# Vision tower on one Trainium2 core: TensorE's fused stage as a loop over two pairs, gelu into its own tile, spectra of the rows loaded for two pairs

## The chip, the cores and the metric

One core of a Trainium2 chip runs the whole program. The metric is the device time of one execution in microseconds, as the median of several runs. "PE" is TensorE (matmuls; "PEld" its weight loads), "DVE" VectorE, "ACT" ScalarE, "POOL" GpSimd, "SP" SyncE, which here only issues transfers.

## The reference

The input is a batch of 64 images of 64 x 64 pixels with 3 channels. The first block is a Fourier network of width 64 with four layers. Around it follow a linear attention, a mixture of experts, a second attention and a second mixture of experts on the tokens; the change does not touch those. Each of the four layers computes, cut to what matters:

```
xf  = rfft2(h)                                   # h: [b, 64, 64, 64]
top = einsum('bixy,ioxy->boxy', xf[:, :, :16, :16], w1)
bot = einsum('bixy,ioxy->boxy', xf[:, :, -16:, :16], w2)
sc  = irfft2(of)                                 # of: zeros, with top and bot in place
pw  = einsum('bihw,oi->bohw', h, pw_w[l]) + pw_b[l]
y   = sc + pw
h   = gelu(batchnorm(y))                         # over batch and pixels, for each channel
```

After the last layer comes `gelu(h @ fc1_w + fc1_b) @ fc2_w + fc2_b`, which gives one number for each pixel.

## The kernel before

All transforms are matmuls with small constant matrices in float32. A layer has two stages. The **mix** stage takes the spectra of all images, 8 chunks of modes one after the other, multiplies them with the layer's weights and stores the products in `spec_out` (in DRAM). It also gathers the sums for the batch norm from the spectra, so that scale and shift are known before any pixel is.

The **fused** stage (`sync_fuse`, `tensor_fuse`, `scalar_fuse`, `vector_fuse`) goes over the 32 pairs of images (`NP = 32`). For each pair it has these steps, each of the pixel steps in four quarters T = 0 to 3:

- `rows` (matmuls on L896, two halves, `hc` 0 and 1): inverse transform over the rows, read from the tile `grp`, transposed by `turn_rows` (DVE, L915) into `a2`.
- `y_of` with `spectral` (L906): inverse transform over the columns; in layer 0 with the pointwise part of the input on top (L1037); in layers 1 and 2 `add_p` (DVE, L923) adds the pointwise part, which was loaded from `y_dram`.
- `gelu` (ACT, L1132 in layer 0, L1135 later), with the batch norm as scale and shift, in place in the pair's tile `pb`.
- `px_turn` (DVE, L1185) transposes it into `hT`; `next_of` (PE, L1064) multiplies it with the next layer's pointwise weights; `evict` (ACT, L1142) copies that result over the gelu in `pb`; `square` (ACT, L1149) sums its squares; SP stores it to `y_dram` (L943, four transfers of 512 KB).
- `w_dft` (L1077), `w_turn`, `h_dft` (L1090), `h_turn` (L1204): the forward transform, whose result SP stores for every four pairs (`store_spectra`, L972, four transfers of 512 KB).

The order is written out by hand on each engine, and the engines meet at semaphores. On PE the loop over the pairs is unrolled in Python; the only loop of the program is the one over layers 1 and 2 (L2418 on PE). In PE's step n the order is: `next_of(n-1, 2)`, `y_of(n, 0)`, `y_of(n, 1)`, `rows_of(n+1, 0)`, `h_dft(n-2)`, `next_of(n-1, 3)`, `y_of(n, 2)`, `rows_of(n+1, 1)`, `w_dft(n-1)`, `next_of(n, 0)`, `next_of(n, 1)`, `y_of(n, 3)`. The half `rows_of(n+1, 1)` waits until `evict` has ended for pair n-1:

```
if hc == 1 and p > 1:
    pe.wait_ge(evicted, n * 4 - 4)
```

SP issues nearly all transfers in one order that is written out too. `grp` has two buffers (`grp[g % 2]`), each for the spectra of a group of four pairs; `load_piece` brings the next group in four pieces of 512 KB, one in each of SP's steps, by way of `load_group`. A step of SP is: a piece of spectra, every fourth time `store_spectra`, then `store(n-1)`, which waits for the same `evicted` count as the half of `rows` above, then `load(n+2)`, a plane of 2 MB from `y_dram` (L876; in layer 0 two transfers of 48 KB from the input, L880).

The last layer (`sync_last`, `tensor_last`) has neither stores nor forward transforms; it goes on to the two layers `fc1` (L1320) and `fc2` (L1332).

Of the kernel before, what the change touches and what calls it, by code (L numbers as in the profile page):

```python
# [114 lines left out]
def build(nc, d, B, out):  # L115
# [5 lines left out]
    with ExitStack() as ctx:  # L121
# [7 lines left out]
        spec_out = nc.dram_tensor("spec_out", [NCH, P, NG, GI * C], F32, kind="Internal").ap()  # L129
# [354 lines left out]
        m_sb = [at(M_AT + u * (2 * B * HB + 8 * BK), NG, 2, GI * HB) for u in range(2)]  # L484
# [44 lines left out]
        def sync_mix(sp, l, first, final=False):  # L529
# [8 lines left out]
            def store(c):  # L538
                sp.wait_ge(mixed_turned, (l * NCH + c) * 4 + 4)
                sp.sem_inc(waited[sp.engine], 1)  # L540
                for t in range(4):
                    row = t % 2 * C + t // 2 * HB
                    if c >= NCH - 2:
                        sp.dma_start(grp[0].rearrange("p (c v) b o -> p c (v b o)", v=2)[row:row + HB, c],
                                     m_sb[c % 2][t * HB:(t + 1) * HB, 0].rearrange("p v x -> p (v x)")).then_inc(grp_loaded[0], 16)
                if c == NCH - 2:
                    for u in range(2):
                        sp.wait_ge(mixed_stored[u], l * (NCH * 32) + (NCH * 32 - 64))
                        sp.sem_inc(waited[sp.engine], 1)
                    load_group(sp, l, 0, slice(0, NCH - 2))  # L550
# [167 lines left out]
        def vector_mix(dve, l, first):  # L718
# [38 lines left out]
            def turn(n):  # L757
# [11 lines left out]
                for j in range(2):  # L769
                    dve.transpose(m_sb[c % 2][:, 4 * j:4 * j + 4, v, :], modes[:, 32 * j:32 * j + 32]).then_inc(mixed_turned, 1)  # L770
# [59 lines left out]
        grp_loaded = [sem("grp_loaded_even"), sem("grp_loaded_odd")]  # L830
# [9 lines left out]
        grp = [at(u * PX, M2, GI, HB) for u in range(2)]  # L840
# [28 lines left out]
        GRP_LOADS = [(NG // 2 - 1) * Q + 9, NG // 2 * Q]  # L869

        def grp_count(l, g):

            return l * (GRP_LOADS[g % 2] * 16) + ((g // 2 * Q + (9, Q)[g % 2]) * 16)

# [8 lines left out]
        def load_piece(sp, l, n):  # L883
            if n // Q + 1 < NG:
# [1636 lines left out]
```

## Time and profile before

| what | value |
|---|---|
| median of 3 runs | 4079.1 us (4076.56 to 4083.73) |
| the profiled execution's own time | 4098.0 us |
| its span, first to last instruction | 4096.2 us |
| mean granted TensorE clock | 0.909 of full |
| PE busy | 3206.6 us (78%) |
| PE weight loads busy | 1856.2 us (45%) |
| DVE busy | 2414.7 us (59%) |
| ACT busy | 2249.3 us (55%) |
| data moved by the queue that SP fills | 774.61 MB, 61.9% of 16 engines' span |

The times of the runs and the profiled execution are not the same execution: durations below are of the profiled one. The page of the profile shows busy time for each engine and groups of instructions by line. The fused stages lie at 264 to 904 us (layer 0), 1120 to 1737 (layer 1), 1953 to 2569 (layer 2) and 2782 to 3379 (last layer), the mix stages ahead of each. In a timeline a row stands for instructions of one kind that follow each other; in brackets is how long the engine stood idle before the row and what ended that. "issue" means that nothing the profile shows was waited for. The count behind the x is in hardware instructions: one float32 matmul of the code is two of them, so a half of `rows` is 8 matmuls in the code and 16 in the trace.

### The profile page before, as it was taken

What the parts mean: (1) busy time and instruction counts of PE and PEld (TensorE: products, weight loads), DVE (VectorE), ACT (ScalarE), POOL (GpSimd) and SP (SyncE); (2) the same over time, 40 slices, a digit from 0 to 9 for tenths busy, and PEclk for the clock granted to TensorE, in tenths of its full rate; (3) what the DMA queues carried; (4) which work ended last, traced back from release to release, by engine and by line L of the source; (5) the groups of instructions that cost most, each with busy time, mean ns of one, the idle gap of its engine ahead of it and who ended that gap; (6) DMA issues with size and microseconds to landing.
All of it is one profiled execution on the core that took longest, in us unless ns stands there. A gap on an engine that the chain in (4) does not pass through costs nothing. (4 is left out here: it accounts for less than half of the span.)

```text
span 4096.2 us, 119274 instructions
## 1 busy us (share of the span) xinstructions
PE 3206.6 (78%) x52804; PEld 1856.2 (45%) x52804; DVE 2414.7 (59%) x2482; ACT 2249.3 (55%) x2652; POOL 173.7 (4%) x249
## 2 busy tenths in 40 slices
PE   6678888886677777867777777678999994869786
PEld 4544444444544444446444444464444442733532
DVE  4555555555677778856778877564333333554556
ACT  3655565665566566656656666565666663222321
POOL 2013200000000000000000000000010012000000
PEclk9899999998899999988899999898999997779688
DMA  8877766668878889888889988886434320011062
GB/s 284 321 207 184 180 157 154 166 159 296 282 246 257 259 237 279 240 308 297 247 240 273 280 253 230 291 303 219 168 127 162 131 86 12 1 43 42 1 118 60
DMA packets 174127, 798.69 MB, mean 195 GB/s; under 512 B 32137, under 2 KB 38609, under 8 KB 124270
## 3 DMA queue, kind: packets, MB, share of 16 engines
q1 hardware_dynamic: 161628, 774.61, 61.9%
q0 software_dynamic: 7936, 13.65, 1.1%
q8 instruction: 425, 6.96, 0.7%
q10 hardware_dynamic: 4050, 2.74, 0.2%
q14 instruction: 88, 0.72, 0.1%
HBM read 445.01 MB, written 342.23 MB: 192 GB/s over the span
## 5 line engine op out<-in xcount | busy, mean ns | idle before, releaser
L906 PEld LDWEIGHTS bank<-fb,arena 64*64 64x64 f32 x16384 | 558.6, 196 | 548.1 <-issue 491.7
L906 PE MATMUL bank<-fb,arena 64*64 64x128 f32 x16384 | 622.6, 290 | 201.3 <-issue 146.5
L923 DVE TENSOR_TENSOR arena<-bank,arena 128x1024 f32<-128x1024 f32 x384 | 467.7, 1218 | 426.6 <-PE bank L906 425.9
L1142 ACT ACTIVATE arena<-bank 128x1024 f32<-128x1024 f32 x384 | 384.0, 1023 | 535.0 <-PE bank L1064 313.3
L1185 DVE STREAM_TRANSPOSE arena<-arena 128x1024 f32<-128x1024 f32 x384 | 458.4, 1212 | 136.7 <-ACT arena L1132 134.8
L915 DVE STREAM_TRANSPOSE arena<-bank 128x1024 f32<-128x1024 f32 x256 | 318.7, 1245 | 327.7 <-PE bank L896 327.4
L1064 PE MATMUL bank<-arena,wst 64*64 64x512 f32 x3072 | 420.1, 631 | 24.3 <-issue 16.6
L1149 ACT ACTIVATE arena<-arena 128x1024 f32<-128x1024 f32 x384 | 403.1, 1050 | 0.3
L1135 ACT ACTIVATE arena<-arena,shift,scale 128x1024 f32<-128x1024 f32 x256 | 316.5, 1236 | 116.1 <-DVE arena L923 114.4
L896 PE MATMUL bank<-arena,ga 64*64 64x256 f32 x4096 | 304.2, 405 | 94.4 <-DVE arena L923 28.4
L637 PE MATMUL bank<-arena 64*64 64x128 f32 x8192 | 276.0, 282 | 92.9 <-issue 63.8
L1090 PE MATMUL bank<-arena,ghq 32*64 32x256 f32 x6144 | 235.6, 419 | 94.4 <-issue 83.2
L637 PEld LDWEIGHTS bank<-arena 64*64 64x64 f32 x8192 | 249.5, 140 | 130.3 <-issue 128.2
L1320 PE MATMUL bank<-arena,fc 64*128 64x512 f32 x1024 | 274.6, 635 | 18.9 <-ACT arena L1388 18.9
L1388 ACT ACTIVATE arena<-bank,fc1b 128x1024 f32<-128x1024 f32 x256 | 272.3, 1101 | 19.6 <-PE bank L1320 19.5
L896 PEld LDWEIGHTS bank<-arena,ga 64*64 64x64 f32 x4096 | 166.4, 139 | 214.4 <-issue 146.4
L754 DVE SCALAR_TENSOR_TENSOR arena<-bank,arena 128x1024 f32<-128x1024 f32 x128 | 156.3, 1223 | 178.0 <-ACT arena L696 177.4
L1380 ACT ACTIVATE arena<-arena,shift,scale 128x1024 f32<-128x1024 f32 x128 | 158.8, 1241 | 183.1 <-DVE arena L923 183.1
L1204 DVE STREAM_TRANSPOSE arena<-bank 128x512 f32<-128x512 f32 x192 | 196.9, 1106 | 98.3 <-PE bank L1090 98.2
L1077 PE MATMUL bank<-arena,fwq 32*32 32x512 f32 x6144 | 240.0, 609 | 16.1 <-issue 13.6
L1192 DVE STREAM_TRANSPOSE arena<-bank 128x1024 f32<-128x1024 f32 x192 | 231.7, 1220 | 21.7 <-PE bank L1077 21.7
L615 PE MATMUL bank<-arena,wst 64*64 64x256 f32 x1536 | 161.4, 447 | 105.4 <-ACT arena L676 73.8
(240 smaller groups left out, 3641.2 us busy)
## 6 DMA issues: line engine op xcount, KB each, us to landing
y_dram<-arena SPq DMA_DIRECT2D x384, 512.0 KB, 8.2
arena<-y_dram SPq DMA_DIRECT2D x96, 2048.0 KB
spec_out<-arena SPq DMA_DIRECT2D x128, 512.0 KB, 10.6
arena<-in_w_modes SPq DMA_DIRECT2D x28, 2048.0 KB, 14.9
arena<-spec_out SPq DMA_DIRECT2D x112, 512.0 KB, 10.9
arena<-spec_in SPq DMA_DIRECT2D x24, 2048.0 KB, 9.7
spec_in<-arena SPq DMA_DIRECT2D x96, 512.0 KB, 8.4
spec_in<-arena SPq DMA_DIRECT2D x8, 2048.0 KB, 13.4
```

The lines of the kernel that those rows point to most:

```text
L637: mm = pe.matmul(bank[4 * v + q][ROW[h], k * 2 * B:(k + 1) * 2 * B], w_sb[c % 3][ROW[row], mode, :], z[ROW[row], :, :, mode, :], start=(sw ...
L896: mm = pe.matmul(bank[2 * s + v][CHAN[par], :].rearrange("p (c r k) -> p r k c", c=16, r=2)[:, r], ga[k_p, r * S:(r + 1) * S], grp[p // Q ...
L906: mm = pe.matmul(hpx(bank[2 * s + i][CHAN[v], :])[:, :, j * S:(j + 1) * S], a2[p % 2][CHAN[i], :, v, 4 * T + j], hpx(fb2[CHAN[i], :]), sta ...
L915: dve.transpose(a2[p % 2].rearrange("p (v c) a m -> p v (c a m)", v=2)[:, :, hc * 512:(hc + 1) * 512], slot(s)).then_inc(rows_turned, 1)
L923: dve.tensor_tensor(chunk(p, T), slot(s), chunk(p, T), ALU.add).then_inc(y_added, 1)
L1064: mm = pe.matmul(bank[2 * NEXT_SLOT[T] + v][CHAN[i], :], wst[CHAN[v], :], pb[p % NS][CHAN[v], i, T * BK:(T + 1) * BK], start=True, stop=Tr ...
L1135: act.activation(chunk(p, T), chunk(p, T), ACT.Gelu, bias=shift[:], scale=scale[:]).then_inc(h_made, 1)
L1142: act.activation(chunk(p, T), slot(NEXT_SLOT[T]), ACT.Copy).then_inc(evicted, 1)
L1149: act.activation(junk_p.rearrange("p (i x) -> p i x", i=2), chunk(p, T), ACT.Square, accum_out=acc[:, p * 4 + T:p * 4 + T + 1]).then_inc(s ...
L1185: dve.transpose(hT[p % 2].rearrange("p i h s c -> p i (h s c)")[:, :, T * BK:(T + 1) * BK], chunk(p, T)).then_inc(px_turned, 1)
L1320: mm = pe.matmul(bank[2 * FC_SLOT[i] + v], fc1[CHAN[v], :], pb[p % NS][CHAN[v], i, T * BK:(T + 1) * BK], start=True, stop=True)
L1388: act.activation(gb[m % NB_G], slot(FC_SLOT[i]).rearrange("p a b -> p (a b)"), ACT.Gelu, bias=fc1b[:]).then_inc(fc1_gelu, 1)
```

## The change

- PE's steps are put in a function `step(m, u)` for pair 2m + u. In layers 1 and 2 the steps of m = 1 to 14 are one loop on the engine, whose body holds two pairs; the first and last steps and all of layer 0 stay unrolled.
- `gelu` writes to a tile of its own, `h_at` (`hidden_of(T)`), which takes the place of the second buffer of `grp`. `next_of` and `px_turn` read it there. `evict` no longer waits for `px_turn`; `gelu` waits for `px_turn` and `next_of` of the pair before.
- `grp` has one buffer, for two pairs. `next_rows` loads it in each second step of SP in one transfer of 1 MB, after `rows` has ended for the two pairs that lie in it. `spec_out` is laid out by pairs, so that a run is 1 KB instead of 2 KB. The mix stage's transposes write `m_sb` in that order.
- At the end of a layer the weights of the next layer's first chunk are issued a step later, after the last `rows`; those of the second chunk after the last stores.

The same on the last layer: it uses `next_rows` and the new `rows`.

```diff
-        spec_out = nc.dram_tensor("spec_out", [NCH, P, NG, GI * C], F32, kind="Internal").ap()
+        spec_out = nc.dram_tensor("spec_out", [NCH, P, NP, 2 * C], F32, kind="Internal").ap()
...
             def store(c):
                 sp.wait_ge(mixed_turned, (l * NCH + c) * 4 + 4)
                 sp.sem_inc(waited[sp.engine], 1)
-                for t in range(4):
-                    row = t % 2 * C + t // 2 * HB
-                    if c >= NCH - 2:
-                        sp.dma_start(grp[0].rearrange("p (c v) b o -> p c (v b o)", v=2)[row:row + HB, c],
-                                     m_sb[c % 2][t * HB:(t + 1) * HB, 0].rearrange("p v x -> p (v x)")).then_inc(grp_loaded[0], 16)
+                if c >= NCH - 2:
+                    for t in range(4):
+                        row = t % 2 * C + t // 2 * HB
+                        sp.dma_start(grp[row:row + HB, c],
+                                     m_sb[c % 2][t * HB:(t + 1) * HB, 0:2].rearrange("p q v x -> p q (v x)")).then_inc(grp_loaded, 16)
                 if c == NCH - 2:
                     for u in range(2):
                         sp.wait_ge(mixed_stored[u], l * (NCH * 32) + (NCH * 32 - 64))
                         sp.sem_inc(waited[sp.engine], 1)
-                    load_group(sp, l, 0, slice(0, NCH - 2))
+                    load_rows(sp, 0, slice(0, NCH - 2))
                 for t in range(4):
...
-                    dve.transpose(m_sb[c % 2][:, 4 * j:4 * j + 4, v, :], modes[:, 32 * j:32 * j + 32]).then_inc(mixed_turned, 1)
+                    dve.transpose(m_sb[c % 2][:, 16 * j:16 * j + 16, v, :].rearrange("p (g q) (a o) -> p g a q o", q=Q, a=2),
+                                  modes[:, 32 * j:32 * j + 32]).then_inc(mixed_turned, 1)
...
-        grp = [at(u * PX, M2, GI, HB) for u in range(2)]
+        grp = at(0, NCH, 2, 2 * C)
+        h_at = at(PX, 2, PX // 2)
...
+        hidden_of = lambda T: h_at[:, :, T * BK:(T + 1) * BK]
...
-        def load_group(sp, l, g, cs):
-
-            if g > 1:
-                sp.wait_ge(rows_done, (l * NP + (g - 1) * Q) * 2)
+        def load_rows(sp, m, cs):
+
+            sp.dma_start(grp[:, cs].rearrange("p c u x -> p c (u x)"),
+                         spec_out[cs, :, 2 * m:2 * m + 2].rearrange("c p u x -> p c (u x)")).then_inc(grp_loaded, 16)
+
+        def next_rows(sp, l, n):
+            if n % 2 == 1 and n + 1 < NP:
+                sp.wait_ge(rows_done, (l * NP + n + 1) * 2)
                 sp.sem_inc(waited[sp.engine], 1)
-            sp.dma_start(grp[g % 2].rearrange("p (c v) b o -> p c (v b o)", v=2)[:, cs],
-                         spec_out[cs, :, g].rearrange("c p x -> p c x")).then_inc(grp_loaded[g % 2], 16)
-
...
-        def load_piece(sp, l, n):
-            if n // Q + 1 < NG:
-                load_group(sp, l, n // Q + 1, slice(n % Q * (NCH // Q), (n % Q + 1) * (NCH // Q)))
-
-        def rows(pe, l, p, hc, s):
-            q = p % Q
-            if hc == 0 and q == 0:
-                pe.wait_ge(grp_loaded[p // Q % 2], grp_count(l, p // Q))
...
-                        mm = pe.matmul(bank[2 * s + v][CHAN[par], :].rearrange("p (c r k) -> p r k c", c=16, r=2)[:, r],
-                                       ga[k_p, r * S:(r + 1) * S], grp[p // Q % 2][k_p, :, par * Q + q, hc * 16:(hc + 1) * 16],
+                        mm = pe.matmul(bank[2 * s + v][CHAN[par], :].rearrange("p (c r k w) -> p r k w c", c=16, r=2, w=2)[:, r],
+                                       ga[k_p, r * S:(r + 1) * S],
+                                       grp[k_p, :, u].rearrange("p k (w a o) -> p k w a o", w=2, a=2)[:, :, :, par, hc * 16:(hc + 1) * 16],
...
-            load_piece(sp, l, 0)
             for n in range(NP + 2):
-                if n + 1 < NP:
-                    load_piece(sp, l, n + 1)
+                next_rows(sp, l, n)
                 if n > 1 and (n - 2) % Q == Q - 1:
                     store_spectra((n - 2) // Q)
-                if n == NP - 2:
+                if n == NP - 1:
+                    sp.wait_ge(rows_done, (l * NP + NP) * 2)
+                    sp.sem_inc(waited[sp.engine], 1)
                     load_modes(sp, l + 1, 0)
                     if first:
                         sp.wait_ge(even_stored, 16 * N_EVEN * L)
                     load_even(sp, l + 1)
                 if n == NP:
-                    sp.wait_ge(rows_done, (l * NP + NP) * 2)
-                    sp.sem_inc(waited[sp.engine], 1)
-                    load_weights(sp, l + 1, 1)
                     sp.wait_ge(y_done, (l * NP + NP) * 4)
                     sp.sem_inc(waited[sp.engine], 1)
                     load_weights(sp, l + 1, 2)
                 if 0 < n <= NP:
                     store(n - 1)
+                if n == NP:
+                    sp.wait_ge(px_turned, (l * NP + NP) * 4)
+                    sp.sem_inc(waited[sp.engine], 1)
+                    load_weights(sp, l + 1, 1)
                 if n + 2 < NP:
                     load(n + 2)
...
-                        mm = pe.matmul(bank[2 * NEXT_SLOT[T] + v][CHAN[i], :], wst[CHAN[v], :], pb[p % NS][CHAN[v], i, T * BK:(T + 1) * BK],
+                        mm = pe.matmul(bank[2 * NEXT_SLOT[T] + v][CHAN[i], :], wst[CHAN[v], :], hidden_of(T)[CHAN[v], i],
...
+            def step(m, u, now=True, before=True, after=True, older=True):
+                last = (m - 1, 1) if u == 0 else (m, 0)
+                then = (m, 1) if u == 0 else (m + 1, 0)
+                if before:
+                    next_of(*last, 2)
+                if now:
+                    y_of(m, u, 0)
+                    y_of(m, u, 1)
+                if after:
+                    rows_of(*then, 0)
+                if older:
+                    h_dft(m - 1, u)
...
...
+            step(0, 0, before=False, older=False)
+            step(0, 1, older=False)
+            if first:
+                for m in range(1, NP // 2 - 1):
+                    for u in range(2):
+                        step(m, u)
+            else:
+                with pe.Fori(1, NP // 2 - 1) as m:
+                    for u in range(2):
+                        step(m, u)
+            step(NP // 2 - 1, 0)
+            step(NP // 2 - 1, 1, after=False)
+            step(NP // 2, 0, now=False, after=False)
+            step(NP // 2, 1, now=False, before=False, after=False)
...
+                if p > 0:
+                    act.wait_ge(px_turned, n * 4 + T - 3)
+                    act.wait_ge(next_done, n * 4 + T - 3)
+                    act.sem_inc(waited[act.engine], 1)
                 if first:
                     act.wait_ge(y_done, n * 4 + T + 1)
-                    act.activation(chunk(p, T), slot(Y_SLOT[T]), ACT.Gelu, bias=shift[:], scale=scale[:]).then_inc(h_made, 1)
+                    act.activation(hidden_of(T), slot(Y_SLOT[T]), ACT.Gelu, bias=shift[:], scale=scale[:]).then_inc(h_made, 1)
                 else:
                     act.wait_ge(y_added, n * 4 + T + 1)
-                    act.activation(chunk(p, T), chunk(p, T), ACT.Gelu, bias=shift[:], scale=scale[:]).then_inc(h_made, 1)
+                    act.activation(hidden_of(T), chunk(p, T), ACT.Gelu, bias=shift[:], scale=scale[:]).then_inc(h_made, 1)
...
-                act.wait_ge(px_turned, n * 4 + T + 1)
+                act.wait_ge(h_made, n * 4 + T + 1)
```

How the rows move on SP, in the fused stage of layers 1 and 2. Before, each step of SP has a piece of spectra (L866), the stores of a pair (L943) and the load of a plane (L876); ISA and REGISTER_ALU are register work:

```order
L876 DMA arena<-y_dram 128x4096 [waits p_stored3,squared]
L866 DMA arena<-spec_out 128x2x512 [waits rows_done]
L939 ISA
L943 DMA y_dram<-arena 64x2048 [waits evicted]
L943 DMA y_dram<-arena 64x2048 x3
L948 REGISTER_ALU
L876 DMA arena<-y_dram 128x4096 [waits p_stored0,squared]
L864 ISA
L866 DMA arena<-spec_out 128x2x512 [waits rows_done]
```

Of the change, at the same place: the transfer of spectra stands once for two steps, it is `128x8x256` (1 MB) in place of `128x2x512`, and the stores of the spectra (L974) follow it.

```order
L878 DMA arena<-y_dram 128x4096 [waits p_stored2,squared]
L871 ISA
L866 DMA arena<-spec_out 128x8x256 [waits rows_done]
L974 DMA spec_in<-arena 32x8x512 [waits hdft_turned]
L974 DMA spec_in<-arena 32x8x512 x3
L941 ISA
L945 DMA y_dram<-arena 64x2048 [waits evicted]
L945 DMA y_dram<-arena 64x2048 x3
L878 DMA arena<-y_dram 128x4096 [waits p_stored3,squared]
```

The stores (L945) and loads (L878) keep their order; the load of spectra moved from one in each step to one in every second, still behind a plane's load.

On PE, the matmuls keep their order. What is new there is the wait for `grp_loaded` at the first half of `rows` of each even pair (before: of each fourth pair), and the jump at the end of the body, behind `y_of(m, 1, 3)` and ahead of `next_of`; the rows of the change, from the body of the loop:

```order
L908 MATMUL bank<-fb,arena 64x2x64 x15
L1013 ISA
L891 ISA [waits y_added]
L897 MATMUL bank<-arena,ga 64x16x16 [waits grp_loaded]
L897 MATMUL bank<-arena,ga 64x16x16 x7
...
L908 MATMUL bank<-fb,arena 64x2x64 [waits evicted]
L908 MATMUL bank<-fb,arena 64x2x64 x15
L1142 REGISTER_ALU
L1142 COMPARE_AND_BRANCH
L1056 ISA
L1065 REGISTER_ALU [waits h_made]
L1074 MATMUL bank<-arena,wst 64x512 [waits evicted]
```

Behind the jump (L1142) the rows of the steps that stay unrolled follow; before, the same matmuls stood there without a jump.

## Rows read from the trace of the kernel before

**Rows 1.** The page: span; the queue that brings instructions (packets, MB, share)

```profile
span 4096.2 us, 119274 instructions
...
q8 instruction: 425, 6.96, 0.7%
```

**Rows 2.** Windows (layer 0, 1, last): us, then PE, PEld, DVE, ACT, POOL; PEclk, DMA, GB/s

```profile
264.00:904.00 640.00, 542.41 (x10594) 303.43 (x10594) 343.26 (x308) 386.14 (x482) 71.46 (x73) 0.98 0.67 165
1120.00:1737.00 617.00, 486.65 (x9602) 275.32 (x9602) 481.94 (x430) 389.97 (x481) 0.37 (x1) 0.93 0.85 252
...
2782.00:3379.00 597.00, 574.28 (x6848) 253.35 (x6848) 234.33 (x203) 397.01 (x366) 55.49 (x112) 0.98 0.40 145
```

**Rows 3.** PE's timeline, layer 1: start us, us, engine line op [idle before]

```profile
1525.64 1.09 PE L896 MATMUL bank<-arena,ga 64*64 64x256 f32 x16 [0.40 <-ACT arena L1142]
...
1536.55 1.09 PE L896 MATMUL bank<-arena,ga 64*64 64x256 f32 x16 [0.51 <-DVE arena L923]
...
1541.89 1.09 PE L896 MATMUL bank<-arena,ga 64*64 64x256 f32 x16 [0.40 <-ACT arena L1142]
```

**Rows 4.** PE's timeline, layer 1: second half of rows of pair 1 and pair 31

```profile
1131.76 1.09 PE L896 MATMUL bank<-arena,ga 64*64 64x256 f32 x16
...
1737.42 1.09 PE L896 MATMUL bank<-arena,ga 64*64 64x256 f32 x16 [0.40 <-ACT arena L1142]
```

**Rows 5.** Timeline of PE's weight loads around one stop, layer 1

```profile
1501.33 0.40 PEld L1077 LDWEIGHTS bank<-arena,fwq 32*32 32x32 f32 x13 [0.32 <-issue]
1505.13 0.24 PEld L1077 LDWEIGHTS bank<-arena,fwq 32*32 32x32 f32 x18 [3.40 <-issue]
```

**Rows 6.** Window between the ends of two stops (columns of rows 2)

```profile
1496.00:1505.10 9.10, 6.23 (x124) 3.10 (x124) 6.63 (x6) 4.34 (x6) 0.00 (x0) 0.98 0.93 279
```

**Rows 7.** The loop's jump, PE (L2418), POOL (L2459): ns min/median/max, first and last start

```profile
L2418 PEldq COMPARE_BRANCH  x2: 83/3246/6410, 1777.5 to 2607.1; - x2
...
L2459 POOLq COMPARE_BRANCH  x2: 40/45/50, 1135.6 to 1967.8; - x2
```

**Rows 8.** SP's timeline, layer 1: when transfers are issued

```profile
1525.59 5.49 SPq L943 DMA_DIRECT2D y_dram<-arena  x4
...
1533.55 2.28 SPq L866 DMA_DIRECT2D arena<-spec_out  x1
...
1559.71 5.37 SPq L972 DMA_DIRECT2D spec_in<-arena  x4
1565.28 9.38 SPq L943 DMA_DIRECT2D y_dram<-arena  x4
```

**Rows 9.** The piece issued at 1533.55 (us to landing); all pieces of layer 1

```profile
arena<-spec_out SPq DMA_DIRECT2D x1, 512.0 KB, 12.6
...
DMA to landing us min/median/max: 7.1/12.1/20.9
```

**Rows 10.** Window of the old piece's transfer, layer 1 (columns of rows 2)

```profile
1541.50:1544.00 2.50, 2.08 (x44) 1.10 (x50) 2.50 (x4) 1.28 (x4) 0.00 (x0) 1.00 0.93 320
```

**Rows 11.** Layer 0: PE's rows, SP's issues, the piece's us to landing

```profile
739.86 1.10 PE L896 MATMUL bank<-arena,ga 64*64 64x256 f32 x16
...
754.47 1.09 PE L896 MATMUL bank<-arena,ga 64*64 64x256 f32 x16
...
759.76 5.49 SPq L943 DMA_DIRECT2D y_dram<-arena  x4
...
769.52 0.63 SPq L866 DMA_DIRECT2D arena<-spec_out  x1
...
arena<-spec_out SPq DMA_DIRECT2D x1, 512.0 KB, 5.7
```

**Rows 12.** Last layer: PE's rows, and the piece issued at 3086.78

```profile
3090.28 1.09 PE L896 MATMUL bank<-arena,ga 64*64 64x256 f32 x16
...
3103.42 1.09 PE L896 MATMUL bank<-arena,ga 64*64 64x256 f32 x16
...
arena<-spec_out SPq DMA_DIRECT2D x1, 512.0 KB, 8.9
```

More of the change, by code:

```diff
@@ L483, in build @@
         r_sb = [at(R_AT + u * B * MC, NG, MC * GI) for u in range(2)]
-        m_sb = [at(M_AT + u * (2 * B * HB + 8 * BK), NG, 2, GI * HB) for u in range(2)]
+        m_sb = [at(M_AT + u * (2 * B * HB + 8 * BK), NP, 2, 2 * HB) for u in range(2)]
         x2 = [at(X_AT + 4 * BK * v, 4 * BK) for v in range(2)]
@@ L881, in load_x, with inner, rows @@
                              ).then_inc(p_loaded[p % NS], 16)
-        def load_piece(sp, l, n):
-            if n // Q + 1 < NG:
-                load_group(sp, l, n // Q + 1, slice(n % Q * (NCH // Q), (n % Q + 1) * (NCH // Q)))
-        def rows(pe, l, p, hc, s):
-            q = p % Q
-            if hc == 0 and q == 0:
-                pe.wait_ge(grp_loaded[p // Q % 2], grp_count(l, p // Q))
+        def inner(m):
+            return not isinstance(m, int)
+        def rows(pe, l, m, u, hc, s):
+            if hc == 0 and u == 0:
+                pe.wait_ge(grp_loaded, l * (GRP_LOADS * 16) + (m * 16 + 9 * 16))
                 pe.sem_inc(waited[pe.engine], 1)
@@ L1032, in y_of @@
                 pe.sem_inc(waited[pe.engine], 1)
-                mm = spectral(pe, p, T, Y_SLOT[T], not first)
+                mm = spectral(pe, u, T, Y_SLOT[T], not first)
                 if first:
@@ L1090, in h_dft @@
                             mm = pe.matmul(bank[4 + c][CHAN[v], 256:512], ghq[QUAD[c], k * 2 * K1:(k + 1) * 2 * K1],
-                                           t1[p % 2][QUAD[c], hh * 2 + v, :, :, ri * M2:(ri + 1) * M2],
+                                           t1[u][QUAD[c], hh * 2 + v, :, :, ri * M2:(ri + 1) * M2],
                                            start=(k == 0), stop=(k == 3), tile_position=(32 * c, C * v))
                 mm.then_inc(hdft_done, 1)
+            def step(m, u, now=True, before=True, after=True, older=True):
[10 more added lines that the diff above has]
+                    h_dft(m - 1, u)
+                if before:
+                    next_of(*last, 3)
+                if now:
+                    y_of(m, u, 2)
+                if after:
+                    rows_of(*then, 1)
+                if before:
+                    w_dft(*last)
+                if now:
+                    next_of(m, u, 0)
+                    next_of(m, u, 1)
+                    y_of(m, u, 3)
@@ L1095, in tensor_fuse @@
             pe.wait_ge(mixed_turned, (l * NU + NU - 1) * 2)
             pe.sem_inc(waited[pe.engine], 1)
[L1097 removed]
+            rows_of(0, 0, 0)
             tensor_sums(pe, l)
[L1099 to L1122 removed]
+            rows_of(0, 0, 1)
@@ L1184, in px_turn @@
                     dve.wait_ge(wdft_done, n - 1)
-                dve.transpose(hT[p % 2].rearrange("p i h s c -> p i (h s c)")[:, :, T * BK:(T + 1) * BK], chunk(p, T)).then_inc(px_turned, 1)
+                dve.transpose(hT[p % 2].rearrange("p i h s c -> p i (h s c)")[:, :, T * BK:(T + 1) * BK], hidden_of(T)).then_inc(px_turned, 1)
             def w_turn(p, i):
@@ L1295, in rows_of @@
                     pe.wait_ge(rows_turned, R + 1)
-                rows(pe, l, p, hc, 0)
+                rows(pe, l, p // 2, p % 2, hc, 0)
             def y_of(p, T):
```

94 lines of the change are left out of this document (36 added, 58 removed).

## The prediction

> **What bounds the kernel now.** I read the stages first, then TensorE's own stream, then the queue that issues the transfers, then the transfers. The profiled execution spans 4096.2 us and took 4098.0 [rows 1]. The stages that the change touches are the fused ones: layer 0 (264 to 904 us), layer 1 (617 us; layer 2 repeats it) and the last layer (597 us) [rows 2]. In layer 1 no engine is full (PE 487 of 617, DVE 482, ACT 390) and the DMA share is 0.85; in the last layer PE is busy 574 of 597 us and the DMA share is only 0.40. So layers 1 and 2 hold waits, the last layer almost none.
>
> Where they are is seen in PE's stream. The matmuls of rows, second half ("hc1"), start once in each pair. An undisturbed step in layer 1 runs from 1525.64 to 1541.89, 16.25 us; in it the first half of the next pair ("hc0") comes at 1536.55, 10.9 us after hc1, and the next hc1 follows 5.3 us after that [rows 3]. But from pair 1 (1131.76) to pair 31 (1737.42) 30 steps took 605.7 us, 20.2 each [rows 4]. The missing 3.9 us a step are stops in the middle of a group of like matmuls, where nothing is awaited: at 1501.33 13 weight loads of the W transform go, then 3.40 us of "issue", then the other 18 [rows 5]. Between the ends of two such stops lie 124 matmuls and 124 loads, and some waits [rows 6], and the instruction queue brought 425 packets with 6.96 MB, 16.4 KB each, which is 256 instructions of 64 bytes [rows 1]. I read this as: PE waits for its code, one packet per 256 instructions, whenever that packet is late behind data. A pair is 320 matmuls and 320 loads, so it needs 2.5 packets.
>
> **The change, part by part.**
>
> *The loop.* Two pairs, some 1,330 instructions, become the body of a loop that 28 of the 32 pairs of layers 1 and 2 run through. If the chip keeps this code over the jump, the 3.9 us go: 28 x (16.3 - 20.2) = -109 us per layer. Whether it keeps it no row shows directly. The nearest two are jumps: POOL's back to the start of a body of a handful of instructions took 40 to 50 ns; PE's, back over a whole layer, took 6410 ns when taken and 83 ns when not [rows 7]. In number of instructions 1,330 lies nearer to the first. I take it as kept, with the other as a rival. Entering and leaving the loop I cost at one late packet, 6 us per layer; extra register work lies ahead of matmuls already queued, nothing.
>
> *The rows' spectra.* This is the part that costs. Before, two buffers hold four pairs each, and pieces of 0.5 MB arrive a group ahead; nothing waits for them. Now one buffer holds two pairs, and its next load waits until PE has done hc1 of the second of them, while PE asks for the result at the next hc0, 10.9 us later by rows 3 (I use 11.2, since other steps take slightly more). The queue serves in order of issue, as I read it, and on SP this load stands behind four stores (2 MB together) and one plane load (2 MB); these are released by the same event as hc1 (the eviction that ends the pair before). In that same step the stores are issued from 1525.59 and the piece of spectra at 1533.55 [rows 8]; it landed 12.6 us after its issue, at 1546.2, that is 20.6 us after the event; over the stage this time to landing is 7.1/12.1/20.9 (least, median, most) [rows 9]. So with the old 0.5 MB it would already be 9 us late. The new load has 1 MB. The queue moved 320 GB/s while the old piece was its last work [rows 10], so 0.5 MB more is 1.6 us if bytes count; if packets of half the length cost as much as long ones, 1 MB takes four times the old piece's 2.5 us, +7.5. I take +2.0, near the former, since in that row the 16 engines are what is full (share 0.93). Landing: 20.6 + 2.0 = 22.6 us after the event, a wait of 22.6 - 11.2 = 11.4 us at hc0. By the Trainium skill's "Advanced Engine Details and Errata", section Clock Domains, an unobstructed descriptor of 1 KiB takes 42 to 43 ns; an estimate from it is 1024 x 43 ns / 16 = 2.8 us for the load, 1.2 us more than the 1.6 us of the old piece's bytes, which would make the wait 10.6 us; no run here shows this size on that queue.
>
> In half of the rounds it is worse. Every fourth pair the four stores of the transformed spectra (2 MB) come between: issued at 1559.71 they hold SP 5.4 us, and the next plane stores go out only at 1565.28 [rows 8]. 2 MB at 320 GB/s is 6.6 us. In the new order they become ready when hc0's stop ends, so the stores, the load and the next spectra all shift back by about 6.6 us: a wait of 18.0 us.
>
> Per layer 14 loads are waited for (pairs 4, 6, ... 30; the first one, for pair 2, has no stores ahead): 8 of them at 11.4, 6 at 18.0 = 199 us. DMA is not full then: two pairs move 10.5 MB, which at 252 to 320 GB/s [rows 2, 10] is 33 to 42 us of the 44 to 51.
>
> Sum for layers 1 and 2: 28 x 16.3 + 199 = 655 us where 28 x 20.2 = 566 stood, +89, and 6 for the loop's ends: +95 per layer, +190.
>
> *Layer 0* has no loop, so its code waits stay. Its plane loads are tiny, so only 2 MB of stores stand ahead: event at 759.8, piece issued at 769.52, landed 5.7 us on, 15.5 us after the event; hc0 is due 14.6 us after hc1 (739.86, 754.47) [rows 11]. With 2.0 us more it lands at 17.5: a wait of 2.9, 14 times = +41 us.
>
> *Last layer.* No stores. hc0 comes 13.1 us after hc1 starts (3090.28, 3103.42), and a piece behind a whole 2 MB load landed in 8.9 us [rows 12]. Now it goes ahead of the plane load: in time. The plane load is issued some 5 us later, a step before its use. 0.
>
> *Gelu into its own tile.* Same instructions; eviction no longer waits for the transpose, gelu waits for last pair's transpose and matmul, done most of a step before. DVE has 482 of 617 us. 0; if that cover went (gelu late by a semaphore), some 0.1 us in each step, 6 us.
>
> *Matmuls, transposes, the end of a layer.* The rows' matmuls keep count and columns, the mix's transposes theirs: 0. Weights for the next layer's first chunk go out one step later, those for its second one behind the last stores, of which the first costs and the second helps by up to one 2 MB transfer (6.6 us) per layer: 0, within 20 either way for all three.
>
> Total: 4098.0 + 190 + 41 = 4329. The runs shown have a median of 4079.1, 19 below the profiled one: **4310 us**.
>
> **The rivals.**
>
> *Code is fetched in the loop too.* For it: so little code is held ahead that a stop follows when one packet is late [rows 5, 6]; and the one long jump of PE cost 6.4 us [rows 7]. The Trainium skill says so in "Runtime: NRT & Kernel Launch", section Instruction fetch mechanics: a taken branch whose target lies outside the two current pages of 256 instructions has to wait for a fetch; in "Advanced Engine Details and Errata", section ISA Cache, it gives TensorE 128 KB in place of 32, which would hold the body, and then says there are only two lines. This trace agrees with the first on PE's long jump and is silent on the second. Price from rows: each round of two pairs has 6.4 us for the jump and of the 7.8 us of code waits the part outside hc1 to hc0 (two thirds, 5.2; the rest is hidden in the wait for spectra), 11.6; the slower round gives the queue time to catch up, -6.6 every second one, so about 8 x 28 rounds = +225: 4535 us, slower.
>
> *The spectra arrive in time: faster.* If the queue does not serve in order of issue, so that the 1 KB packets pass the 16 KB ones of the plane load, the load is there by hc0. Then -109 + 6 per layer and nothing in layer 0: 4310 - 190 - 41 - 206 = 3873 us. It decides where the waits of a layer sum to under 103 us, 7.4 per load, a landing by 18.6 us after the event. For it: the least time to landing is 7.1 us [rows 9]. Against it: the median is 12.1, and a small piece took 12.6 behind a load but 5.7 where none was ahead [rows 9, 11].
>
> *The late spectra hide in other waits: no change.* With a wait near 7.4 us gain and loss cancel: 4079, within 8 (0.2%, about what a measurement of this kernel can tell from no change).
>
> **How the numbers follow.** First case 0.53, own range 4150 (the new load as short as the old piece, no shift by the stored spectra: 14 x 9.4 = 132 in place of 199 per layer, and 0.9 in place of 2.9 in layer 0) to 4540 (short packets cost as much as long ones: +5.5 us x 42). Code fetched: 0.28, 4450 to 4620. In time: 0.13. No change: 0.04. Slower by less than the first case's low end: 0.02. The predicted time is the first case's; 4150 to 4590 leaves out the fast cases and the tips of the others, 2 in 10. Faster 0.14, same 0.04, slower 0.82.
>
> **What would show it.** In the profile after: TensorE's hc0 in layers 1 and 2 waits for the DMA from spec_out 14 times per layer, 11 or 18 us each; rounds of 44 and 51 us; the instruction queue's packets fall by some 140 (56 pairs of 2.5), and no stop inside a group in the loop. Packets unchanged and a stop of 6 us at the jump: the first rival. No wait at hc0 and steps of 16 to 18 us: the second, and my reading of the queue as in order is what failed. Layer 0 longer by some 41 us, the last layer within 5.

## The result and the profile after

The changed kernel takes 4332.8 us (median of 4 runs, 4324.5 to 4339.1) where the kernel before takes 4078.0 beside it: a ratio of 1.062 (95% interval 1.060 to 1.064). The forecast was 4310 us, slower.

The page of the changed kernel: the span, the instruction queue, the rows' matmuls, the load of their spectra.

```profile
span 4326.6 us, 120049 instructions
...
q8 instruction: 291, 4.77, 0.4%
...
L897 PE MATMUL bank<-arena,ga 64*64 64x256 f32 x4096 | 316.7, 427 | 467.0 <-DMA arena<-spec_out 395.9
...
arena<-spec_out SPq DMA_DIRECT2D x60, 1024.0 KB, 10.7
```

The span is 230 us longer than in [rows 1] (the medians are 255 apart). TensorE is idle 396 us ahead of the rows because of the load from `spec_out`, the wait that the kernel before did not have. The instruction queue brings 291 packets instead of 425. In layer 1 the line of the rows says how often it waits, and the loop's jump (L1142) what it costs:

```profile
L897 PE MATMUL bank<-arena,ga x1024: 375/377/687, 1150.0 to 1867.8; 64*64 64x256 f32 x171
its engine sat idle before it (us, times) until:
  issue: 222.8, 82
  DMA arena<-spec_out: 182.5, 14
```

```profile
L1142 PEldq COMPARE_BRANCH  x28: 76/210/247, 1236.8 to 2783.8; - x28
```

The 14 waits sum to 182.5 us. The jump is met 28 times in the two layers, 14 in each; 26 times it is taken, at 0.2 us each. The stages, as windows of the changed kernel (layer 0, layer 1, last layer; columns of rows 2):

```profile
261.00:901.00 640.00, 527.04 (x10022) 289.22 (x10022) 326.30 (x293) 365.57 (x458) 71.35 (x73) 0.95 0.64 157
1152.00:1867.00 715.00, 471.37 (x9602) 269.17 (x9602) 479.93 (x431) 390.22 (x482) 0.37 (x1) 0.86 0.74 218
3011.00:3608.00 597.00, 573.76 (x6848) 253.37 (x6848) 234.44 (x203) 396.18 (x366) 55.25 (x112) 0.98 0.41 147
```

Layer 1 now takes 715 us for the work that took 617 [rows 2]; the DMA share fell from 0.85 to 0.74, so over the stage the rate of the transfers was not the limit. The last layer has not moved. (In the 640 us of layer 0 fewer matmuls fall than in [rows 2]: that stage grew too.) From pair 1 to pair 31, second half of rows to second half of rows, the 30 steps take:

| stage | before | after | difference | forecast |
|---|---|---|---|---|
| layer 0 | 628.3 | 665.7 | +37 | +41 |
| layer 1 | 605.7 [rows 4] | 703.8 | +98 | +95 |
| layer 2 | 604.9 | 701.8 | +97 | +95 |
| last layer | 577.1 | 577.4 | 0 | 0 |

The sum of the differences, 232 us, is the whole difference of the spans within 2 us, so the ends of the layers and the mix stages cost nothing. One late load, in the timeline of the changed kernel (start us, length, engine line op, idle before):

```profile
1201.06 5.48 SPq L945 DMA_DIRECT2D y_dram<-arena  x4
1206.67 2.39 SPq L878 DMA_DIRECT2D arena<-y_dram  x1
1209.59 1.83 SPq L866 DMA_DIRECT2D arena<-spec_out  x1
...
1222.68 1.99 PE L897 MATMUL bank<-arena,ga 64*64 64x256 f32 x16 [9.37 <-DMA arena<-spec_out]
1224.60 3.71 PE L1100 MATMUL bank<-arena,ghq 32*64 32x256 f32 x64
...
1230.68 0.66 PE L897 MATMUL bank<-arena,ga 64*64 64x256 f32 x8 [0.40 <-ACT arena L1172]
1241.63 1.09 PE L897 MATMUL bank<-arena,ga 64*64 64x256 f32 x16 [0.52 <-DVE arena L925]
1242.66 1.98 PE L1100 MATMUL bank<-arena,ghq 32*64 32x256 f32 x64
...
1246.97 1.09 PE L897 MATMUL bank<-arena,ga 64*64 64x256 f32 x16 [0.41 <-ACT arena L1172]
```

The four plane stores go out at 1201.06 (the event), the plane load at 1206.67, the spectra at 1209.59, and TensorE starts at 1222.68, 21.6 us after the event. The lines behind it hold what no term of the forecast had: after the wait the same 16 matmuls take 1.99 us instead of 1.09 and the 64 of the H transform 3.71 instead of 1.98. From hc0 to hc1 (first and second half of the rows of one pair) it takes 8.0 us here, and 5.3 one step later. Windows over that place show the granted clock (before the wait, in it, twice behind it):

```profile
1204.00:1213.00 9.00, 8.04 (x181) 4.32 (x156) 7.73 (x8) 7.44 (x10) 0.00 (x0) 1.00 0.96 227
1213.00:1222.60 9.60, 0.31 (x12) 0.12 (x7) 2.94 (x3) 3.37 (x4) 0.00 (x0) 0.77 0.80 296
1222.60:1227.50 4.90, 4.82 (x72) 2.84 (x80) 2.38 (x2) 0.00 (x0) 0.00 (x0) 0.50 0.01 3
1227.50:1231.00 3.50, 3.10 (x64) 1.64 (x52) 2.58 (x3) 1.49 (x2) 0.00 (x0) 0.88 0.00 0
```

It fell during the idle wait and stood at 0.50, the lower of its two levels (1.2 of 2.4 GHz), for the first 4.9 us of work after it. The DMA share is 0.01 there, so no transfer slows these matmuls. Over the 14 waits of layer 1 the mean from hc0 to hc1 is 7.5 us, 2.1 more than 5.3.

### The profile page after: what moved, and what is told of

It reads as the page before. It is cut to its first block and busy times, and to the rows that moved or that the text cites. A ratio compares the mean times of both kernels' runs of the same rounds, so it can differ in the third digit from the quotient of the medians.

```text
span 4326.6 us, 120049 instructions
## 1 busy us (share of the span) xinstructions
PE 3189.8 (74%) x52804; PEld 1844.6 (43%) x52804; DVE 2410.4 (56%) x2482; ACT 2247.1 (52%) x2652; POOL 173.3 (4%) x249
## 5 line engine op out<-in xcount | busy, mean ns | idle before, releaser
L908 PEld LDWEIGHTS bank<-fb,arena 64*64 64x64 f32 x16384 | 544.7, 196 | 506.0 <-issue 449.7
L908 PE MATMUL bank<-fb,arena 64*64 64x128 f32 x16384 | 602.7, 288 | 166.8 <-issue 96.6
L897 PE MATMUL bank<-arena,ga 64*64 64x256 f32 x4096 | 316.7, 427 | 467.0 <-DMA arena<-spec_out 395.9
L1074 PE MATMUL bank<-arena,wst 64*64 64x512 f32 x3072 | 402.4, 611 | 12.5 <-DMA wst<-in_pw_t 7.2
L1087 PE MATMUL bank<-arena,fwq 32*32 32x512 f32 x6144 | 225.6, 598 | 5.5 <-issue 3.8
```

The source lines that it names most:

```text
L897: mm = pe.matmul(bank[2 * s + v][CHAN[par], :].rearrange("p (c r k w) -> p r k w c", c=16, r=2, w=2)[:, r], ga[k_p, r * S:(r + 1) * S], gr ...
L908: mm = pe.matmul(hpx(bank[2 * s + i][CHAN[v], :])[:, :, j * S:(j + 1) * S], a2[u][CHAN[i], :, v, 4 * T + j], hpx(fb2[CHAN[i], :]), start=( ...
L1074: mm = pe.matmul(bank[2 * NEXT_SLOT[T] + v][CHAN[i], :], wst[CHAN[v], :], hidden_of(T)[CHAN[v], i], start=True, stop=True, tile_position=( ...
```

## The experiments

My theory: the late load of spectra costs all of the loss and more, the loop gains something beside it, and of the late load what counts is its lead (11 us from release to need) against a landing some 21 us after the event. Rivals: the loop itself costs; the gelu's tile or the 1 KB runs cost; the bytes of the transfers bind. All times below are medians with their ratio to the kernel before on the same chip and its interval.

**1 to 3. Loop and place of the load, each alone.** `early_loop` issues the load ahead of the stores and the plane load:

```diff
 for n in range(NP + 2):
-    next_rows(sp, l, n)
+    if n == 1:
+        next_rows(sp, l, n)
...
     if 0 < n <= NP:
+        next_rows(sp, l, n + 1)
         store(n - 1)
```

> The changed kernel with one edit on SP: from pair 2 on, the load of the spectra for the next two pairs is issued ahead of the four stores and the plane load that the same event releases, instead of behind them. Theory 1 (the lateness is the place in the queue): the load goes out about 1.2 us after the event and lands within 9 us of it, ahead of the first half of rows at 11.2 us; the 14 waits per layer fall from 182 us to under 20. Steps in layers 1 and 2 are then 16.3 us if PE sets them (some 3875 us in all) or about 17.8 us if the transfers do, at a DMA share near 1 (some 3960 us). Rival (the transfer itself is too long, or the queue does not serve in order of issue): most of the waits stay and the time is above 4200 us.

`late_unrolled` is the changed kernel with the loop written out (`if True:` for `if first:` at the loop), `early_unrolled` has both edits.

> The changed kernel with TensorE's loop over two pairs unrolled in layers 1 and 2, all else as in the change. If the loop is what took the code waits away: the instruction queue's packets go back from 291 to about 425, stops inside groups return; of the 7.8 us of such waits in a round of two pairs some 5 lie outside the wait for spectra, 28 x 5 = 140 us, less what the queue catches up in them: 4380 to 4480 us. Rival (the stops had another cause, which the new tile or order removed): packets rise, but time stays within 20 us of 4333.

> Both edits: spectra loaded ahead of the stores, TensorE unrolled. If the change consists of just two effects, the loop's gain and the late spectra, this kernel has neither and should be the kernel before again: steps of 20.2 us on average in layers 1 and 2, 425 packets of code, 4050 to 4110 us. If the new tile for gelu or the 1 KB runs cost or gain something of their own, it shows here as a difference from 4078.

| | loop | written out |
|---|---|---|
| load late (as changed) | 4332.8, 1.062 [1.060, 1.064] | 4363.2, 1.069 [1.066, 1.071] |
| load first | 3964.4, 0.969 [0.966, 0.973] | 4086.3, 1.001 [0.998, 1.004] |

With both undone the kernel is the one before, within its interval, and both versions that are written out bring 425 packets of code again: the gelu's tile, the 1 KB runs and the new layout, taken together, cost and bring nothing that can be measured. The late load alone costs 277 us, the loop alone gains 122. Together they do not add: beside late spectra the loop gains only 30. Layer 1 of `late_unrolled` shows why:

```profile
L897 PE MATMUL bank<-arena,ga x1024: 375/377/687, 1151.0 to 1886.5; 64*64 64x256 f32 x171
its engine sat idle before it (us, times) until:
  issue: 194.1, 77
  DMA arena<-spec_out: 148.5, 14
```

The same 14 waits are 148.5 us there instead of 182.5. Part of the stops for code falls into the wait for spectra, so that taking them away mostly lengthens that wait: from pair 1 to pair 31 layer 1 took 722.8 us written out and 703.8 with the loop, 19 less, while the waits grew by 34. My expectation of 4380 to 4480 had too little of this. In `early_loop` the wait is almost gone; its layer 1, the same 9602 matmuls, as a window and as the line's waits:

```profile
1122.00:1674.00 552.00, 454.15 (x9602) 262.34 (x9602) 477.71 (x431) 389.99 (x481) 0.37 (x1) 0.96 0.90 282
```

```profile
who waited for it (us, times):
  PE bank L897: 26.7, 5
...
DMA to landing us min/median/max: 6.6/8.4/15.0
```

The load lands 8.4 us after its issue (median) and TensorE waits 5 times, 26.7 us in all. This version beats both kernels.

**4. Does the loop's body fit?** `early_four` has four pairs in the body, some 2,660 instructions. Its jump is met 14 times in the two layers and taken 12 times.

```diff
-with pe.Fori(1, NP // 2 - 1) as m:
-    for u in range(2):
-        step(m, u)
+with pe.Fori(0, NP // 4 - 1) as k:
+    for j in range(2):
+        for u in range(2):
+            step(k * 2 + (1 + j), u)
```

> As early_loop, but the body of TensorE's loop holds four pairs, about 2660 instructions instead of 1330, in 7 rounds instead of 14. If the chip keeps a body of that length over the jump: packets of code as in early_loop (about 290) and the time within 10 us of it. If it does not: packets near 425, a jump that takes about 6 us in each of 14 rounds, +84 us, and code waits as in early_unrolled: 4130 to 4180 us. By the Trainium skill, page Runtime: NRT & Kernel Launch, section Instruction fetch mechanics, TensorE holds 2048 instructions, which the body of 1330 fits and that of 2660 does not; what stands there of a window of two pages would have forbidden the first as well.

4196.1 us, 1.028 [1.024, 1.032]. Its page, its jump, and TensorE's timeline at the first jump:

```profile
q8 instruction: 445, 7.29, 0.7%
```

```profile
L1144 PEldq COMPARE_BRANCH  x14: 83/6948/7560, 1231.4 to 2648.0; - x14
```

```profile
1231.02 1.19 PE L908 MATMUL bank<-fb,arena 64*64 64x128 f32 x32 [0.45 <-ACT arena L1175]
...
1238.94 1.99 PE L1076 MATMUL bank<-arena,wst 64*64 64x512 f32 x8 [6.73 <-issue]
```

A body of 2,660 instructions is fetched anew in each round (445 packets, more than the 425 of [rows 1]) and a taken jump costs 6.2 to 7.6 us (median of all 14: 6.9), near the 6.4 of [rows 7]. Against `early_unrolled` with its 425 packets it is 110 us slower by the medians, 7.8 us for each of its 14 rounds. A body of 1,330 is kept: 291 packets and 0.2 us. So my first rival described a body of twice the size. The Trainium skill, "Runtime: NRT & Kernel Launch", section Instruction fetch mechanics, has a taken branch wait when its target lies outside two pages of 256 instructions; our trace of 26 taken jumps back over 1,330 instructions in 0.2 us each disagrees with that.

**5, 6. Place in the queue, or lead?** `pair_late` leaves the load at the changed kernel's late place, but brings it pair by pair (0.5 MB, runs of 512 B) into the half of the tile that is free, so that each has a step more, some 16 us, between its release and its first use; `pair_early` also issues it first.

```diff
-    if n % 2 == 1 and n + 1 < NP:
+    if n + 2 < NP:
...
-        load_rows(sp, (n + 1) // 2, slice(0, NCH))
+        sp.dma_start(grp[:, :, n % 2],
+                     spec_out[:, :, n + 2].rearrange("c p x -> p c x")).then_inc((grp_loaded, grp_odd)[n % 2], 16)
```

> The spectra of rows come pair by pair (0.5 MB each, runs of 512 B): the half of the tile that belongs to a pair is refilled as soon as that pair's second half of rows is done, at the same place in SP's order as in the changed kernel (behind the stores and the plane load), and it is wanted a whole step later than there. If the wait at hc0 is a matter of slack (a landing some 20 us after the event against 11 us of lead), the lead is now 27.5 us: the waits go also where the stored spectra stand ahead (landing about 27), steps come to the 16.7 us of the kernel that issues the load first, 3955 to 3990 us. If the place in the queue itself is what costs (the load delays what stands behind it), no better than 4250. If packets of half the length cost as much as long ones (57 ns, as 1 KB took, instead of 29), 0.25 MB-worth of extra queue time per pair, some 1.8 us in each step where transfers are full: 4060 to 4090.

> As pair_late, and each pair's load stands ahead of the plane stores and the plane load. If only slack matters, the same as pair_late within 10 us, since that one has enough; if pair_late still waits in the rounds with stored spectra, this one is faster than it by up to 6 x 6.6 us per layer.

`pair_late` takes 3961.1 us, 0.969 [0.966, 0.973], as fast as `early_loop`; `pair_early` 3983.4, 0.976 [0.973, 0.979], a little slower than either. Layer 1 of `pair_late` (line of the rows, at L902 in it):

```profile
  DMA arena<-spec_out: 20.8, 6
```

Same place, same stores and plane load ahead of it, 20.8 us of waits in place of 182.5. What costs is a lead shorter than the time to landing; the place in the queue matters only where the lead is that short. Packets of 512 B show no penalty: in layer 1 of this trace they took 27 ns each (median), where the 1 KB packets of the changed kernel took 46.

**7, 8. The gelu's tile.** `evict_waits` (on the changed kernel) and `early_evw` (on `early_loop`) make the eviction wait for the transpose again, as before the change.

```diff
-act.wait_ge(h_made, n * 4 + T + 1)
+act.wait_ge(px_turned, n * 4 + T + 1)
 act.wait_ge(next_done, n * 4 + T + 1)
```

> The changed kernel with one edit: the eviction waits again for the transpose of the hidden tile, as in the kernel before, so the gelu's tile of its own decouples nothing. If the decoupling costs and brings nothing, as forecast, the time is that of the changed kernel, 4320 to 4340 us. If an earlier eviction is what moved the stores up, each pair's event comes up to 1.2 us (one transpose) later and the wait with it: 14 to 28 waits per layer, up to 4400.

> The loop with the load issued first (3964 us) and the eviction waiting again for the transpose. Where transfers bind, the same within 10 us; if the decoupling carried part of that gain, 3990 to 4030.

4327.2 us, 1.061 [1.058, 1.064], and 3964.7 us, 0.972 [0.969, 0.975]: each the same as its kernel without the edit, within the interval. The decoupling costs nothing and brings nothing that can be measured.

**9, 10. The clock after a wait.** If the clock falls because TensorE is idle, work in the wait must keep it. Both kernels add matmuls on old data, once per round, ahead of the wait for the spectra (17 groups of four in `warm_wait`, 10 in `warm_short`):

```diff
+if hc == 0 and u == 0 and inner(m):
+    for _ in range(17):
+        for i in range(2):
+            for v in range(2):
+                pe.matmul(bank[v][CHAN[i], :], wst[CHAN[v], :], idle[CHAN[v], :],
+                          start=True, stop=True, tile_position=(v * C, i * C))
 rows(pe, l, m, u, hc, ROWS_SLOT[hc])
```

> The changed kernel; in the loop, between the wait for the slot and the wait for the spectra of rows (once per round), TensorE does 68 more matmuls of 64x64 by 64x512 on old data, into the bank that the rows overwrite next. At their rate in this kernel (402 us for 3072 of them, 131 ns each) they fill 8.9 of the 9.4 us, and of the 15.9 us, that it otherwise waits idle. Their result is not used; nothing is left out. If the rows after a wait are slow because the granted clock had fallen while TensorE was idle, they run at full rate again in at least the 8 shorter waits of each layer: 16 x 2.5 us = 40 us less (4290), up to 70 less if it holds in the long waits too. If they are slow for another reason (the transfer in flight), no change: 4320 to 4345. If the added work isn't hidden, or lowers the clock elsewhere, slower than 4345.

`warm_wait`: 4387.5 us, 1.075 [1.071, 1.078]. I had sized the work wrongly: a matmul in the code is two records in the trace.

```profile
1264.86 14.82 PE L1024 MATMUL bank<-arena,wst 64*64 64x512 f32 x136 [0.51 <-DVE arena L926]
1279.47 1.07 PE L898 MATMUL bank<-arena,ga 64*64 64x256 f32 x16
1280.47 1.98 PE L1107 MATMUL bank<-arena,ghq 32*64 32x256 f32 x64
...
1284.79 1.09 PE L898 MATMUL bank<-arena,ga 64*64 64x256 f32 x16 [0.41 <-ACT arena L1179]
```

The added work lasts over 14 us, past the landing, and costs 55 us net (by the two ratios, 51). But behind it the rows stand at the fast value (1.07, 1.98, hc0 to hc1 in 5.3 us), behind all 14 loads of layer 1 and 13 of the 14 of layer 2. So once more, shorter:

> As the run before with added matmuls in the wait, but of the right length: there 68 matmuls took 14.2 us (each is two records in the trace, which its expectation had overlooked), longer than the shorter waits, and its rows behind them ran at full rate (5.3 us from hc0 to hc1, where the changed kernel takes 7.0 to 8.0 in layers 1 and 2). Now 40, some 8.4 us, inside every wait of 9.4 us or more. The 2.1 us per wait that the fall of the clock costs, by those rows, comes back in the 8 shorter waits of each layer: 34 us, 4290 to 4305; if the clock also holds through the 7 us that then remain idle in the long waits, 28 x 2.1 = 59 us: 4270 to 4280. If TensorE's work holds up something else, no gain: 4320 or more.

`warm_short`: 4299.3 us, 1.052 [1.047, 1.056], 34 us less than the changed kernel (by the two ratios, 42) though TensorE does 2,240 matmul records more. A short wait in its layer 1:

```profile
1253.67 8.81 PE L1024 MATMUL bank<-arena,wst 64*64 64x512 f32 x80 [0.52 <-DVE arena L926]
1264.22 1.09 PE L898 MATMUL bank<-arena,ga 64*64 64x256 f32 x16 [1.73 <-DMA arena<-spec_out]
1265.24 1.98 PE L1107 MATMUL bank<-arena,ghq 32*64 32x256 f32 x64
...
1269.55 0.66 PE L898 MATMUL bank<-arena,ga 64*64 64x256 f32 x8 [0.40 <-ACT arena L1179]
```

The granted clock behind this wait, as a window:

```profile
1264.20:1269.20 5.00, 4.93 (x120) 3.24 (x120) 3.73 (x4) 0.82 (x1) 0.00 (x0) 1.00 0.00 0
```

It is 1.00 where it was 0.50 behind the wait of 9.4 us, and the DMA share is 0 as it was there. Hc0 to hc1 is 5.3 us again in the short waits and still 6.8 to 8.2 in most of the long ones, where some 3 to 5 us stay idle; the mean of the 14 in layer 1 fell from 7.5 to 6.1. This is shown: in the changed kernel a wait of 9 us or more on TensorE costs the wait and some 2.1 us more.

**11, 12. What is left in `early_loop`.** From pair 5 to pair 30 its steps in layer 1 are 16.3 or 16.7 us except one in four, six in all, of 22 to 24: the one behind the four stores of the transformed spectra. `early_half` loads only half of the channels' spectra (its output is another one; the work of the engines is the same), `early_last` issues those stores behind the plane stores and the plane load.

```diff
-load_rows(sp, (n + 1) // 2, slice(0, NCH))
+load_rows(sp, (n + 1) // 2, slice(0, NCH // 2))
```

> The loop with the load issued first (3964 us), but each load in the fused stages brings only the first half of the channels (0.5 MB in place of 1 MB for two pairs); the other half of the tile keeps old spectra, so the output is another one. The work of all engines is the same. If what is left over the 16.3 us of an undisturbed step (18.0 in layers 1 and 2) is the transfers' rate, 15 x 0.5 MB at some 300 GB/s is 1.7 us in each of 15 rounds, 26 us per layer, 52 in all: 3905 to 3920. If it is the order in which SP waits and issues, nothing: 3955 to 3975.

```diff
-    if n > 1 and (n - 2) % Q == Q - 1:
+    if n == NP + 1:
         store_spectra((n - 2) // Q)
...
     if n + 2 < NP:
         load(n + 2)
+    if 1 < n <= NP and (n - 2) % Q == Q - 1:
+        store_spectra((n - 2) // Q)
```

> The loop with the load issued first, and the four stores of the transformed spectra (2 MB, every fourth pair) issued behind the plane stores and the plane load of their step instead of ahead of everything. In the kernel with the load first, layer 1's steps are 16.3 or 16.7 us but for one in four, which takes 22 to 24: the one behind these stores. If the order of issue is what makes it long, these steps come near 16.7 too: 7 x 5.8 us in each of layers 1 and 2, some 80 us less, 3870 to 3900. If it is their bytes (2 MB at 300 GB/s is 7 us, in a queue that has no slack), the wait moves to the next load: 3950 to 3980. If the next transposes of spectra then wait for the stored ones, slower than 3980.

`early_half`: 3954.0 us, 0.969 [0.966, 0.972], not apart from `early_loop`. Its six long steps in layer 1 take 19.0 to 22.2 us, and from pair 1 to pair 31 it is 8 us shorter in layer 1 and 2 in layer 2, where 26 were expected if the rate of the transfers bound: three steps in four have nothing to win from fewer bytes, and the fourth wins little. In these steps the plane is late too, and VectorE waits for it before it adds; layer 1 of `early_loop`, `early_half` and `pair_early`:

```profile
DVE arena L925 <- DMA arena<-y_dram: 18.3, 6, 3.7
...
DVE arena L925 <- DMA arena<-y_dram: 18.2, 7, 3.2
...
DVE arena L930 <- DMA arena<-y_dram: 26.2, 6, 5.1
```

In `pair_early` TensorE waits for no load of spectra at all in layer 1, and the long steps are still 22.1 to 23.9 us. So the late plane alone is enough to make them long.

`early_last`: 4069.6 us, 0.997 [0.995, 0.999], 105 slower than `early_loop`; the waits of its layer 1:

```profile
PE bank L1091 <- DVE arena L1238: 59.2, 6, 10.4
DVE arena L1238 <- DMA spec_in<-arena: 58.5, 6, 10.3
```

The next transpose into the spectra's tile waits 10 us for the stores that still read it, and TensorE behind it. These stores are as urgent as the planes; with one tile for them the fourth step stays long. Whether a second tile would shorten it was not tried.

## Why the prediction was right

**The sum.** The mechanism was forecast, but the closeness of the sum is partly luck: two errors cancelled. Per layer 1 or 2 the forecast had 14 waits of 199 us in all; measured are 182.5 of wait, and 14 x 2.1 = 30 us of low clock behind them that no term had. 30 x 16.3 + 182.5 + 30 = 701.5, against 703.8 measured; of the rest the loop's ends add 8.5 (below) and 14 x 0.4 = 6 go, because the short wait for VectorE ahead of hc0 disappears in the wait for the spectra. Step by step: the eight shorter ones take 27.8 to 29.1 us, the six behind stored spectra 34.1 to 34.9; the forecast's rounds of 44 and 51 us are 16.3 more than these, and came. The forecast's 231 us are set against the profiled executions, which differ by 230; the medians differ by 255, because the profiled execution of the kernel before lay 20 us above its median and that of the changed kernel 4 below. That is why the 4310 falls 23 us short.

**The landing.** Forecast 22.6 us after the event; 21.6 in the timeline above, at the start of TensorE. The added 0.5 MB of 1 KB packets cost little, as bytes at the queue's rate would. My range's upper end, where short packets cost as much as long ones, is excluded: the packets took 46 ns each (median, layer 1), those of 2 KB in the kernel before 84 (its old piece of spectra), and those of 512 B in `pair_late` 27. The estimate from "Advanced Engine Details and Errata", section Clock Domains, in the Trainium skill gave a wait of 10.6 us from 43 ns for 1 KB. The 46 ns measured are near its figure. The eight shorter waits of layer 1 are 9.4 to 11.5 us with a mean of 10.5, nearer to it than to my 11.4; the six longer ones have a mean of 16.4 where 18.0 was forecast.

**The queue in order of issue.** Right: the load came last wherever it was issued last, and 1 KB packets did not pass the plane load. Between the issue of the load above and 1217.0, and in the 5 us from then on, the queues moved:

```profile
DMA packets 190, 2.31 MB, mean 312 GB/s; under 512 B 23, under 2 KB 23, under 8 KB 23
...
DMA packets 1069, 1.28 MB, mean 256 GB/s; under 512 B 31, under 2 KB 1055, under 8 KB 1055
```

In the first 7.4 us there is no packet of 1 KB, in the next 5 all 1,024. This decided against the rival "in time", which `early_loop` made true by issuing the load first and `pair_late` by a longer lead: its arithmetic (14 waits gone, loop kept) gave 3873, measured are 3961 and 3964. It lacked the step behind the stored spectra, in `early_loop` 21.7 to 24.3 us instead of 16.3, six times in each of two layers: 78 us of the some 90.

**The loop.** Kept, as taken (0.53): packets fell by 134 (forecast 140), undisturbed steps are 16.3 us, and the jump takes 0.2. But "-109 us per layer" was never reached: measured with the spectra in time it is 122 us for both layers, since a step in four then waits for transfers, and 30 beside late spectra. In the sum this did no harm, because I set the steps to 16.3 and then added the waits, and did not subtract a gain from the measured total.

**The rest.** Layer 0: +37 for +41; there the 14 waits are 31.1 us. The last layer: 0 as forecast. The gelu's tile: 0, shown by runs 7 and 8. The loop's ends, forecast at 6 us per layer: the steps to pairs 2, 3 and 31 take 19.0, 20.3 and 18.1 us in layer 1 and 18.4, 18.1 and 17.8 in layer 2, over 16.3 each 8.5 and 5.4 us in all.

## What to carry to other kernels

When a buffer is halved, count the lead from its release to its next use and set it against issue to landing, with everything that the same event puts ahead in the queue; if it falls short, load by halves or issue first, since 0.5 MB pieces a step earlier did as well as the best order. Gains that remove stalls on the waiting engine are worth little while a later wait absorbs them: test the loop and the load apart before judging either. Price a wait on TensorE at more than its length if the clock falls in it (here by 2.1 us, behind waits of 9.4 to 17.3 us).

## What was not expected of the hardware

- A wait of 9.4 us left TensorE at half clock (0.50) for the first 4.9 us of work; matmuls took 1.99 us in place of 1.09. Filling most of the wait with unused matmuls made the kernel 34 us faster.
- TensorE keeps a loop body of 1,330 instructions (taken jump 0.2 us, 134 packets saved) and not one of 2,660 (taken jump 6.2 to 7.6 us, 20 packets more than straight code).
- Runs of 512 B were as good as runs of 1 KB for this load: packets of 512 B, 1 KB and 2 KB took 27, 46 and 84 ns (medians).
